# Last stage of a two-layer graph network on Trainium2: three of ten output chunks written by an early store and a later adding transfer

## The chip, the cores and the metric

The kernel runs on one core of one Trainium2 chip. Five engines work side by side and meet through semaphores: TensorE (PE; its weight loads are listed apart as PEld), VectorE (DVE), ScalarE (ACT), GpSimd (POOL) and SyncE (SP), which here only issues transfers. Sixteen DMA engines carry all transfers of the core. The metric is the device time of one execution in microseconds (us), and lower is better.

## The reference

The graph has 1250 nodes of 512 features and 40000 edges. Two residual layers follow each other, cut here to the end of the second, which is what the change touches:

```python
h = max(layernorm(x), 0)
x = x + L0_gnn(h, edges, edge_attr)          # edge MLP, sum over edges, node MLP, affine layernorm
h = max(layernorm(x), 0)
support = (h @ U * s) @ Vt                   # U: 512 x 64, Vt: 64 x 512
gathered = support[src] * edge_weight[:, None]
out = segment_sum(gathered, dst) + bias
x = x + relu(out)
return x                                     # 1250 x 512, fp32
```

## The kernel before, in words

The program is a row of stages, each written once for each engine: a prologue, an edge stage that takes nearly all of the time (to about 1406 us of the trace), a node stage, and a final stage. The 1250 nodes are cut into ten chunks of 128 rows (`NCH` is 10; the last chunk has 98 rows). An engine runs its own part of a stage in the order in which it is written, and waits with `wait_ge` on a semaphore where it needs another engine or a transfer.

The node stage makes `x1`, the input of the second layer, pair of chunks by pair of chunks. `second_norm(p)` on DVE is its last step for the pair p: it raises the semaphore `n_nm` (`s_nm`) by one, after `x1` of chunks 2p and 2p+1 has its final value for this stage. ACT then makes the normed `h2` out of it (L1731), PE multiplies by `U` (L2052) and then by the weighted adjacency `M` (L2065), summed over all ten chunks in two PSUM banks. `M` is loaded from the DRAM table `M_tab` by SP, the last eight chunks of it behind one wait (L1618, tiles `Mb` and `Mc`). When the sum is complete, ACT and DVE copy one half each into the tile `sums` (L1787, L1974).

The final stage computes out = x1 + relu(sums @ Vt + bias) for each chunk. Chunks go in pairs (0,5), (1,6), (2,7), (3,8), (4,9), and `turn` is a chunk's place in that order. PE seeds a PSUM bank with the bias (L2302) and adds the product by `VV` (L2308). Six banks serve the ten turns (`pf`), so the seed of turn 6 waits until the bank of turn 0 has been read, and so on. In `final_stage` DVE takes relu and the sum with `x1` in one instruction (L2292) and SP stores the chunk to `out` (L2327). ACT and GpSimd have nothing to do there.

An adding transfer exists in the kernel already: GpSimd issues `dma_start(..., accum_op=ALU.add)`, which adds the source to what stands at the destination. The edge stage uses it to DRAM (L988, `agg_tab`, 64 KB each; L999, `M_tab`) and the node stage to SBUF (L1663 and L1664, rows of `b4` and `beta` added to the tiles `hb`, `xb`, `uTh_raw` and `ag`). The tile `ag` (four chunks of 128 x 512) is last used in the node stage, for the last pair.

Of the kernel before, what the change touches and what calls it, by code (L numbers as in the profile page):

```python
# [23 lines left out]
ACT = mybir.ActivationFunctionType  # L24
AX = mybir.AxisListType

P = 128
# [3 lines left out]
NCH = -(-N // P)  # L31
# [184 lines left out]
def gnn_two_layers(nc, x, src_idx, dst_rows, src_cols, dst_cols, eaT, ew_cols, W1, b1, W2, b2, W3, b3, W4, b4,  # L216
# [4 lines left out]
    def sem(name):  # L221
        assert name not in names
        names.add(name)
        return ctx.enter_context(nc.semaphore(name))
# [7 lines left out]
    def twice(sb, name, shape):  # L232

        st, sb_raw, _ = scope()
        with st:
            raw = sb_raw(name + "_raw", shape)
        return raw, sb(name, shape, F32R)
# [18 lines left out]
    with ctx:  # L256
# [13 lines left out]
        with st:  # L270
            VV = sb_late("VV", [P, H])
            bhl = sb_late("bhl", [P, H], F32R)
            sums = sb_late("sums", [P, HALFN])
# [11 lines left out]
        with st:  # L285
            V3raw, V3l = twice(sb_late, "V3l", [P, KC, H])
# [4 lines left out]
        ag = sb("ag", [P, 4, H])  # L291
        st, _, ps_node = scope()
        with st:
            pu = [ps_node(f"pu{i}") for i in range(2)]
            pt = [ps_node(f"pt{i}") for i in range(2)]
            pu += [ps_node(f"pu{i}") for i in range(2, 4)]
            po = [ps_node(f"po{i}") for i in range(2)]
        q_w3 = sem("q_w3")
        q_v3 = sem("q_v3")
# [480 lines left out]
        with xst:  # L780
            x1 = sb("x1", [P, NCH, H])
            S = sb("S", [P, NCH, R])
            sel = sb("sel", [P, H], F32R)
            s_sum = sem("k_sum")
            q_v = sem("k_v")
            s_bhl = sem("s_bhl")
            node_stage(node, scope, sem, locals())
            conv_general(c_general, scope, sem, locals())
            final_stage(final, sem, locals())
# [712 lines left out]
def node_stage(work, scope, sem, k):  # L1502
# [3 lines left out]
    ident, iota_p, nTh, nTl, x1, S, sel, ag, q_ag = (  # L1506
        k[n] for n in ("ident", "iota_p", "nTh", "nTl", "x1", "S", "sel", "ag", "q_ag"))
    x, b3, b4, W3, W4, rstd0, nmr0, M_d, Mb, VV, bhl, sums = (
        k[n] for n in ("x", "b3", "b4", "W3", "W4", "rstd", "nmr", "M_d", "Mb", "VV", "bhl", "sums"))
    gamma, beta, U, sv, Vt, bias, row_bcast, newton = (  # L1510
        k[n] for n in ("gamma", "beta", "U", "sv", "Vt", "bias", "row_bcast", "newton"))
    pu, pt, po, xpart, load_ag, s_fin, s_agg, s_t, s_sum, q_v, s_bhl = (
        k[n] for n in ("pu", "pt", "po", "xpart", "load_ag", "s_fin", "s_agg", "s_t", "s_sum", "q_v", "s_bhl"))
    V3raw, V3l, q_v3 = (k[n] for n in ("V3raw", "V3l", "q_v3"))
    NORMS = [(0, 0), (1, 0), (0, 1), (1, 1), (0, 2), (1, 2), (0, 3), (1, 3), (0, 4), (1, 4)]

    st, sb, _ = scope()
    with st:
# [54 lines left out]
        s_ln = sem("n_ln")  # L1573
        s_var = sem("n_var")
        s_r = sem("n_r")
        s_nm = sem("n_nm")
        s_h2 = sem("n_h2")
        s_t2 = sem("n_t2")
        s_e2 = sem("n_e2")
# [682 lines left out]

def final_stage(work, sem, k):

    x1, sums, VV, bhl, sel, out, pu, pt, po, s_sum, q_v, s_bhl = (
        k[n] for n in ("x1", "sums", "VV", "bhl", "sel", "out", "pu", "pt", "po", "s_sum", "q_v", "s_bhl"))
    pf = [pt[0], pt[1], pu[2], pu[3], po[0], po[1]]
    PAIRS = [(i, i + NCH // 2) for i in range(NCH // 2)]
    turn = {c: n for n, c in enumerate(c for pair in PAIRS for c in pair)}
    s_f = sem("k_f")  # L2270
    s_out = sem("k_out")
    q_o = sem("k_o")

    def rows(c):

        return min(P, N - c * P)

    @work.on("scalar")
    def _(e):
        pass  # L2280

    @work.on("gpsimd")
    def _(e):
        pass

    @work.on("vector")
    def _(e):
        for pair in PAIRS:
            for c in pair:
                r = rows(c)  # L2290
                e.wait_ge(s_f, turn[c] + 1)
                e.scalar_tensor_tensor(x1[0:r, c, :], pf[turn[c] % 6][0:r, :], 0.0, x1[0:r, c, :], ALU.max, ALU.add)\  # L2292
                 .then_inc(s_out, 1)

    @work.on("tensor")
    def _(e):
        def seed(pair):
            for c in pair:
                if turn[c] >= 6:
                    e.wait_ge(s_out, turn[c] - 5)  # L2300
                a = R * (c // (NCH // 2))
                e.matmul(pf[turn[c] % 6][0:rows(c), :], sel[a:a + R, 0:rows(c)], bhl[a:a + R, :], start=True, stop=False,  # L2302
                         skip_group_check=True)

        def product(pair):
            for c in pair:
                a, o = R * (c // (NCH // 2)), c % (NCH // 2) * P
                e.matmul(pf[turn[c] % 6][0:rows(c), :], sums[a:a + R, o:o + rows(c)], VV[a:a + R, :], start=False, stop=True,  # L2308
                         skip_group_check=True).then_inc(s_f, 1)

        e.wait_ge(s_bhl, 2)
        e.wait_ge(q_v, 2 * 16)
        for pair in PAIRS[0:3]:
            seed(pair)
        e.wait_ge(s_sum, 2)
        for n, pair in enumerate(PAIRS):
            if n >= 3:
                seed(pair)
            product(pair)

    @work.on("sync")
    def _(e):
        for pair in PAIRS:
            for c in pair:
                r = rows(c)
                e.wait_ge(s_out, turn[c] + 1)
                e.dma_start(out[c * P:c * P + r, :], x1[0:r, c, :]).then_inc(q_o, 16)  # L2327
        e.wait_ge(q_o, 16 * NCH)


# ---- launch: one core; the host only lays the edges out by groups and subtiles
# [32 lines left out]
```

## Time and profile before

| what | us |
|---|---|
| median of 3 runs | 1541.91 |
| lowest and highest of them | 1540.08, 1542.75 |
| the profiled execution, its own time | 1540.79 |
| its span in the trace | 1539.1 |
| PE, DVE, ACT, POOL busy | 1498.8, 1414.7, 1296.5, 1082.4 |

Times in the trace count from the start of the span. An instruction belongs to a line of the kernel (L2292), and `out<-in` names the tiles that it writes and reads. Idle time is shown with what ended it. DMA rows cut a window into 40 equal slices: a digit is the busy share of the 16 DMA engines in tenths, and GB/s is what they moved. Queue q1 holds the transfers that SP issues, q0 those that GpSimd issues.

### The profile page before, as it was taken

Reading aid. Unit: us, or ns where it says so; the run is one execution under the profiler, and the core shown is the slowest. Engines: PE = TensorE matmul, PEld = TensorE weight load, DVE = VectorE, ACT = ScalarE, POOL = GpSimd, SP = SyncE. Lnnn points to the kernel's source line nnn. Section 1 sums busy time; section 2 is a strip of 40 time slices with the busy share of each in tenths; the row PEclk is TensorE's granted clock in tenths of the full one; section 3 lists DMA queues with packets and bytes.
Section 4 is the critical chain, followed back from the end, with each engine's and each line's share of the span. In section 5 each row is a group of like instructions: output and inputs, shape, how many; then the busy total and the mean of one; then the engine's idle time right before and its main releaser. Section 6 shows DMA issues by size and latency. Waiting matters only on the chain.

```text
span 1539.1 us, 33365 instructions
## 1 busy us (share of the span) xinstructions
PE 1498.8 (97%) x7862; PEld 1170.1 (76%) x7862; DVE 1414.7 (92%) x2922; ACT 1296.5 (84%) x2505; POOL 1082.4 (70%) x984
## 2 busy tenths in 40 slices
PE   7969999999999999999999999999999999999998
PEld 5747777777777777777777777777777777776785
DVE  7679999999999999999999999999999999995666
ACT  4058999999999999999999999999999999995462
POOL 1246888888888788787788887888878888762220
PEclk9979999999999999999999999999999999999999
DMA  8845555555554555544554555555555455455673
GB/s 310 306 138 142 125 118 122 124 119 117 124 123 116 123 123 115 127 117 115 126 119 116 127 121 117 121 124 118 118 122 124 116 123 124 112 136 127 137 146 151
DMA packets 122452, 205.10 MB, mean 133 GB/s; under 512 B 31641, under 2 KB 54297, under 8 KB 122416
## 3 DMA queue, kind: packets, MB, share of 16 engines
q0 software_dynamic: 59392, 116.85, 34.8%
q1 hardware_dynamic: 62672, 87.30, 18.2%
q10 hardware_dynamic: 352, 0.52, 0.1%
q8 instruction: 16, 0.26, 0.1%
q14 instruction: 20, 0.16, 0.0%
HBM read 151.60 MB, written 42.75 MB: 126 GB/s over the span
## 4 chain that ended last, share of the span: by engine, by line
PE 81%; issue 5%; DVE 4%; POOL 4%; DMA 3%; ACT 1%; POOLq 1%; DVEq 0%; SPq 0%; ACTq 0%
PE bm L1070 48%; PE bp L1049 6%; PE bp L1057 5%; PE bs L1093 4%; PE bp L1059 4%; PE pu L336 2%; PE pm L1081 2%; PE pu L1998 2%; PE po L2020 2%; PE pB L679 2%; DMA xg<-A_tab,idx 1%; PE pm L1080 1%; POOL hTl L974 1%; POOL M_tab L999 1%; POOL agg_tab L988 1%
## 5 line engine op out<-in xcount | busy, mean ns | idle before, releaser
L974 POOL TENSOR_TENSOR hTl<-tp,hTh 128x512 fp32r<-128x512 f32 (+1 forms) x314 | 411.0, 1309 | 224.5 <-DVE khl L1261 203.5
L1070 PE MATMUL bm<-W2h,hTh 128*128 128x512 f32 x1252 | 498.4, 398 | 2.2 <-POOL hTl L974 1.7
L1070 PE MATMUL bm<-W2l,hTh 128*128 128x512 f32 x1252 | 497.0, 397 | 0.0
L1070 PE MATMUL bm<-W2h,hTl 128*128 128x512 f32 x1252 | 494.5, 395 | 0.0
L963 POOL DMA_INDIRECT xg<-A_tab,idx x305 | 319.4, 1047 | 49.5 <-issue 39.1
L1070 PEld LDWEIGHTS bm<-W2h,hTh 128*128 128x128 f32 x1252 | 235.5, 188 | 71.7 <-DVE bm L1254 14.8
L1131 ACT ACTIVATE rp<-bp 128x512 f32<-128x512 f32 (+1 forms) x314 | 183.3, 584 | 116.8 <-PE bp L1059 115.7
L1070 PEld LDWEIGHTS bm<-W2l,hTh 128*128 128x128 f32 x1252 | 235.6, 188 | 57.5
L1070 PEld LDWEIGHTS bm<-W2h,hTl 128*128 128x128 f32 x1252 | 235.6, 188 | 53.7
L1225 DVE SCALAR_TENSOR_TENSOR rp<-rp 128x512 f32<-128x512 f32 (+1 forms) x314 | 215.6, 687 | 38.7 <-ACT rp L1131 25.8
L1235 DVE SCALAR_TENSOR_TENSOR tp<-rp,bp 128x512 f32<-128x512 f32 (+1 forms) x314 | 211.7, 674 | 4.5 <-ACT rp L1137 2.2
L1248 DVE SCALAR_TENSOR_TENSOR tm<-rm,bm 128x512 f32<-128x512 f32 x313 | 210.5, 673 | 3.4 <-ACT rm L1154 3.4
L1254 DVE COPY bm<-b2b 128x512 f32<-128x512 f32 x309 | 210.7, 682 | 0.0
L1134 ACT ACTIVATE rp<-rp 128x512 f32<-128x512 f32 (+1 forms) x314 | 195.5, 623 | 10.8 <-DVE rp L1225 4.8
L1150 ACT ACTIVATE rm<-rm 128x512 f32<-128x512 f32 x313 | 197.9, 632 | 5.0
L1152 ACT ACTIVATE rm<-rm 128x512 f32<-128x512 f32 x313 | 195.1, 623 | 0.1
L1154 ACT ACTIVATE rm<-rm 128x512 f32<-128x512 f32 x313 | 195.0, 623 | 0.1
L1137 ACT ACTIVATE rp<-rp 128x512 f32<-128x512 f32 (+1 forms) x314 | 194.1, 618 | 0.1
L1146 ACT ACTIVATE rm<-bm 128x512 f32<-128x512 f32 x313 | 185.0, 591 | 1.9 <-DVE tm L1248 1.8
L1049 PEld LDWEIGHTS bp<-ident_r,xg 128*128 128x128 f32 (+1 forms) x1244 | 124.1, 141 | 75.3 <-issue 42.3
L988 POOL DMA_DIRECT2D agg_tab<-ev x157 | 156.4, 996 | 25.2 <-DMA agg_tab<-ev 13.2
L999 POOL DMA_DIRECT2D M_tab<-mev x157 | 163.8, 1044 | 10.1 <-issue 9.2
(244 smaller groups left out, 2318.9 us busy)
## 6 DMA issues: line engine op xcount, KB each, us to landing
ea<-in_eaT SPq DMA_DIRECT2D x156, 128.0 KB
M_tab<-mev POOLq DMA_DIRECT2D x157, 80.0 KB
agg_tab<-ev POOLq DMA_DIRECT2D x157, 64.0 KB
db<-in_dst_rows SPq DMA_DIRECT2D x78, 128.0 KB
M<-M SPq DMA_DIRECT2D x76, 128.0 KB
xg<-A_tab,idx POOLq DMA_INDIRECT x313
eaW<-Bh_tab SPq DMA_DIRECT2D x77, 64.0 KB
eaW<-Bl_tab SPq DMA_DIRECT2D x77, 64.0 KB
```

The lines of the kernel that those rows point to most:

```text
L963: e.indirect_dma_start(out=xg[p][0:r, t, :].bitcast(F32), out_offset=None, in_=A_d, in_offset=bass.IndirectOffsetOnAxis(ap=idx[p][0:r, t:t ...
L974: e.tensor_tensor(hTl[p][:, j, 0:w], pick(u, start_t, tp)[:, 0:w], hTh[p][:, j, 0:w], ALU.subtract)\
L1049: e.matmul(bank[:, t * P:t * P + r].bitcast(F32R), xg[p][0:r, t, j * P:(j + 1) * P], ident_r[0:r, 0:r], start=t == 0, stop=False, is_trans ...
L1070: last = e.matmul(bank[0:r, :], a[p][:, c, j * P:j * P + r], w[:, c, :], start=False, stop=c == KC - 1 and w is W2l, skip_group_check=True)
L1134: e.activation(t, t, ACT.Ln, bias=1.0, scale=0.5 / (SQ * SQ)).then_inc(a_pre, 1)
L1150: e.activation(t, t, ACT.Square, bias=SQ, scale=SQ).then_inc(a_msg, 1)
L1152: e.activation(t, t, ACT.Ln, bias=0.5, scale=0.5 / (SQ * SQ)).then_inc(a_msg, 1)
L1154: e.activation(t, t, ACT.Exp, scale=-1.0).then_inc(a_msg, 1)
L1225: e.scalar_tensor_tensor(t, t, 2.0 * SQ, t, ALU.add, ALU.mult).then_inc(v_sq, 1)
L1235: e.scalar_tensor_tensor(t, pick(u, start_r, rp)[:, 0:w], 1.0, pick(u, start_bank, bp)[:, 0:w], ALU.subtract, ALU.mult).then_inc(v_pre, 1)
L1248: e.scalar_tensor_tensor(tm[m.const % MBUF][0:r, :], rm[m.const % 2][0:r, :], 1.0, bm[m.j][0:r, :], ALU.subtract, ALU.mult).then_inc(v_msg, 1)
L1254: e.tensor_copy(bm[m.j][:, :], b2b[:]).then_inc(v_bias, 1)
```

## The change

For chunks 0, 1 and 2 (`ADDED`) the output is now made in two steps. SP stores `x1` of the three chunks to `out` as it stands, once `n_nm` has reached 2. In the final stage ACT takes the relu of their PSUM banks into the tile `ag`, and GpSimd adds `ag` to `out` with three adding transfers of 256 KB, each behind ACT's relu and the first also behind the landing of the three early stores (`k_x1`). The other seven chunks (`REST`) go as before. A seed that takes over a bank read by ACT waits for ACT instead of DVE.

```diff
+    TURNS = [c for pair in PAIRS for c in pair]
+    ADDED = [0, 1, 2]
+    REST = [c for c in TURNS if c not in ADDED]
...
     @work.on("scalar")
     def _(e):
-        pass
+        for c in ADDED:
+            e.wait_ge(s_f, turn[c] + 1)
+            e.activation(ag[:, c, :], pf[turn[c] % 6][:, :], ACT.Relu).then_inc(s_relu, 1)

     @work.on("gpsimd")
     def _(e):
-        pass
+        e.wait_ge(q_x1, 16 * len(ADDED))
+        for c in ADDED:
+            e.wait_ge(s_relu, c + 1)
+            e.dma_start(out[c * P:(c + 1) * P, :], ag[:, c, :], accum_op=ALU.add).then_inc(q_add, 16)
+        e.wait_ge(q_add, 16 * len(ADDED))
...
     @work.on("tensor")
...
                 if turn[c] >= 6:
-                    e.wait_ge(s_out, turn[c] - 5)
+                    old = TURNS[turn[c] - 6]
+                    if old in ADDED:
+                        e.wait_ge(s_relu, ADDED.index(old) + 1)
+                    else:
+                        e.wait_ge(s_out, REST.index(old) + 1)
...
     @work.on("sync")
     def _(e):
-        for pair in PAIRS:
-            for c in pair:
-                r = rows(c)
-                e.wait_ge(s_out, turn[c] + 1)
-                e.dma_start(out[c * P:c * P + r, :], x1[0:r, c, :]).then_inc(q_o, 16)
-        e.wait_ge(q_o, 16 * NCH)
+        e.wait_ge(s_nm, 2)
+        for c in ADDED:
+            e.dma_start(out[c * P:(c + 1) * P, :], x1[:, c, :]).then_inc(q_x1, 16)
+        for c in REST:
+            r = rows(c)
+            e.wait_ge(s_out, REST.index(c) + 1)
+            e.dma_start(out[c * P:c * P + r, :], x1[0:r, c, :]).then_inc(q_o, 16)
+        e.wait_ge(q_o, 16 * len(REST))
```

DVE's loop runs over `REST` instead of all ten chunks, and is otherwise the same. The rows below are the instructions of an engine in program order; lines marked + have the numbers of the changed kernel, and `k_out` counts DVE's results, `k_relu` ACT's, `k_x1` the landings of the early stores.

SP, from the end of the node stage (the branch of L144) to the end of the program:

```order
 L144 UNCONDITIONAL_BRANCH
-L2327 DMA out<-x 128x512 [waits k_out] x9
-L2327 DMA out<-x 98x512 [waits k_out]
+L2340 DMA out<-x 128x512 [waits n_nm]
+L2340 DMA out<-x 128x512 x2
+L2344 DMA out<-x 128x512 [waits k_out] x6
+L2344 DMA out<-x 98x512 [waits k_out]
 L148 UNCONDITIONAL_BRANCH [waits k_o]
```

Three of SP's ten stores no longer wait for DVE's result; they stand directly behind the loads of `M`, with a wait for `n_nm` alone.

GpSimd, from the end of the node stage to the end of the program (the first rows belong to a branch that is not taken here):

```order
 L2186 DMA h_S<-Sl_tab,h_idx 64x64
 L144 UNCONDITIONAL_BRANCH
+L2295 DMA out<-ag 128x512 [waits k_relu,k_x1]
+L2295 DMA out<-ag 128x512 [waits k_relu] x2
+L148 UNCONDITIONAL_BRANCH [waits k_add]
```

GpSimd gains three transfers and a wait for their landing (`k_add`), ahead of the end of the program.

## Rows read from the trace of the kernel before

**Rows 1.** Chain that ended last, its final pieces: start us, us, what.
```profile
1529.61 4.26 DVE x L2292 x7
...
1534.47 1.20 DVE x L2292 x2
```
**Rows 2.** DMA queues, window 1529 to 1539.1 (the last stage).
```profile
DMA  0000000049999999999999999999999998872000
GB/s 32 0 0 0 0 0 0 0 170 373 389 390 365 406 349 381 381 357 422 357 389 389 365 397 389 381 389 373 397 381 365 381 341 235 260 268 97 0 0 0
q1 hardware_dynamic: 1408, 2.56, 69.9%
```
**Rows 3.** Timeline of the last stage: start us, us, engine, instruction [idle before].
```profile
1528.54 1.02 PE L2308 MATMUL pt<-VV,sums 64*128 64x512 f32 x4
...
1529.59 1.29 DVE L2292 SCALAR_TENSOR_TENSOR x<-pt,x 128x512 f32<-128x512 f32 x2 [1.25 <-PE pt L2308]
1530.25 1.02 PE L2308 MATMUL po<-VV,sums 64*128 64x512 f32 x4
1530.31 5.87 SPq L2327 DMA_DIRECT2D out<-x  x10
...
1532.43 1.04 PE L2308 MATMUL pu<-VV,sums 64*128 64x512 f32 x4
```
**Rows 4.** Windows: us, busy of PE, PEld, DVE, ACT, POOL; then PEclk, DMA share, GB/s.
```profile
1431.00:1436.00 5.00, 5.00 (x31) 4.14 (x30) 3.11 (x6) 4.19 (x8) 1.58 (x2) 1.00 1.09 259
1437.00:1445.00 8.00, 8.00 (x34) 5.92 (x32) 3.68 (x6) 1.92 (x4) 1.30 (x1) 1.00 1.03 187
1474.00:1482.00 8.00, 6.65 (x47) 5.85 (x46) 3.00 (x10) 6.64 (x14) 2.74 (x3) 1.00 1.04 198
1484.50:1490.50 6.00, 6.00 (x42) 5.34 (x41) 3.85 (x12) 0.44 (x3) 0.77 (x1) 1.00 1.04 157
1508.00:1529.00 21.00, 20.71 (x155) 13.37 (x156) 12.17 (x42) 7.85 (x17) 0.00 (x0) 1.00 0.02 8
1531.20:1537.50 6.30, 2.27 (x14) 0.92 (x10) 4.47 (x8) 0.00 (x0) 0.00 (x0) 0.93 1.02 375
```
**Rows 5.** SP's issues before the last stage, and ACT's reads of x of chunks 0 to 3.
```profile
1496.03 2.19 SPq L1618 DMA_DIRECT2D Mc<-M_tab  x4
L1731 ACT ACTIVATE xb<-x,nmr,rstd x4: 802/802/805, 1467.9 to 1474.0; 128x512 f32<-128x512 f32 x4
```
**Rows 6.** Page, part 5: ACT reading a PSUM bank of 128x512.
```profile
L1131 ACT ACTIVATE rp<-bp 128x512 f32<-128x512 f32 (+1 forms) x314 | 183.3, 584 | 116.8 <-PE bp L1059 115.7
```
**Rows 7.** DMA queues (packets, MB, share) in windows 1431:1436, 1437:1445, 1474:1482.
```profile
q0 software_dynamic: 351, 0.72, 78.7%
q1 hardware_dynamic: 127, 0.57, 30.0%
...
q0 software_dynamic: 484, 0.96, 82.6%
q1 hardware_dynamic: 261, 0.51, 19.4%
...
q0 software_dynamic: 572, 1.12, 84.3%
q1 hardware_dynamic: 256, 0.46, 19.4%
```
**Rows 8.** Adding transfers: GpSimd's issue, and issue to landing of agg_tab (to DRAM).
```profile
1482.20 1.19 POOL L1663 DMA_DIRECT2D ag<-in_b  x1 [0.73 <-ACT ag L1701]
...
1483.51 1.76 POOL L1666 DMA_DIRECT2D ag<-in_beta  x1
...
DMA to landing us min/median/max: 4.8/7.6/9.7
```
**Rows 9.** DMA queues, window 1483 to 1492, three adding transfers alone.
```profile
DMA  0000178999799999999899959999999793000000
ag<-in_beta POOLq DMA_DIRECT2D x1, 196.0 KB, 7.6
```

More of the change, by code:

```diff
@@ L786, in gnn_two_layers @@
             s_bhl = sem("s_bhl")
+            s_nm = sem("n_nm")
             node_stage(node, scope, sem, locals())
@@ L1513, in node_stage @@
         k[n] for n in ("pu", "pt", "po", "xpart", "load_ag", "s_fin", "s_agg", "s_t", "s_sum", "q_v", "s_bhl"))
-    V3raw, V3l, q_v3 = (k[n] for n in ("V3raw", "V3l", "q_v3"))
+    V3raw, V3l, q_v3, s_nm = (k[n] for n in ("V3raw", "V3l", "q_v3", "s_nm"))
     NORMS = [(0, 0), (1, 0), (0, 1), (1, 1), (0, 2), (1, 2), (0, 3), (1, 3), (0, 4), (1, 4)]
@@ L1575, in node_stage @@
         s_r = sem("n_r")
-        s_nm = sem("n_nm")
         s_h2 = sem("n_h2")
@@ L2263, in final_stage @@
 def final_stage(work, sem, k):
-    x1, sums, VV, bhl, sel, out, pu, pt, po, s_sum, q_v, s_bhl = (
-        k[n] for n in ("x1", "sums", "VV", "bhl", "sel", "out", "pu", "pt", "po", "s_sum", "q_v", "s_bhl"))
+    x1, ag, sums, VV, bhl, sel, out, pu, pt, po, s_sum, q_v, s_bhl, s_nm = (
+        k[n] for n in ("x1", "ag", "sums", "VV", "bhl", "sel", "out", "pu", "pt", "po", "s_sum", "q_v", "s_bhl", "s_nm"))
     pf = [pt[0], pt[1], pu[2], pu[3], po[0], po[1]]
     PAIRS = [(i, i + NCH // 2) for i in range(NCH // 2)]
-    turn = {c: n for n, c in enumerate(c for pair in PAIRS for c in pair)}
+    TURNS = [c for pair in PAIRS for c in pair]
+    ADDED = [0, 1, 2]
+    REST = [c for c in TURNS if c not in ADDED]
+    turn = {c: n for n, c in enumerate(TURNS)}
     s_f = sem("k_f")
+    s_relu = sem("k_relu")
     s_out = sem("k_out")
+    q_x1 = sem("k_x1")
+    q_add = sem("k_add")
     q_o = sem("k_o")
@@ L2279, in _ @@
     def _(e):
-        pass
+        for c in ADDED:
+            e.wait_ge(s_f, turn[c] + 1)
+            e.activation(ag[:, c, :], pf[turn[c] % 6][:, :], ACT.Relu).then_inc(s_relu, 1)
     @work.on("gpsimd")
     def _(e):
-        pass
+        e.wait_ge(q_x1, 16 * len(ADDED))
[3 more added lines that the diff above has]
+        e.wait_ge(q_add, 16 * len(ADDED))
     @work.on("vector")
     def _(e):
-        for pair in PAIRS:
-            for c in pair:
-                r = rows(c)
-                e.wait_ge(s_f, turn[c] + 1)
-                e.scalar_tensor_tensor(x1[0:r, c, :], pf[turn[c] % 6][0:r, :], 0.0, x1[0:r, c, :], ALU.max, ALU.add)\
-                 .then_inc(s_out, 1)
+        for c in REST:
+            r = rows(c)
+            e.wait_ge(s_f, turn[c] + 1)
+            e.scalar_tensor_tensor(x1[0:r, c, :], pf[turn[c] % 6][0:r, :], 0.0, x1[0:r, c, :], ALU.max, ALU.add)\
+             .then_inc(s_out, 1)
     @work.on("tensor")
@@ L2322, in _ @@
     def _(e):
-        for pair in PAIRS:
-            for c in pair:
-                r = rows(c)
-                e.wait_ge(s_out, turn[c] + 1)
-                e.dma_start(out[c * P:c * P + r, :], x1[0:r, c, :]).then_inc(q_o, 16)
-        e.wait_ge(q_o, 16 * NCH)
+        e.wait_ge(s_nm, 2)
+        for c in ADDED:
+            e.dma_start(out[c * P:(c + 1) * P, :], x1[:, c, :]).then_inc(q_x1, 16)
+        for c in REST:
+            r = rows(c)
+            e.wait_ge(s_out, REST.index(c) + 1)
+            e.dma_start(out[c * P:c * P + r, :], x1[0:r, c, :]).then_inc(q_o, 16)
+        e.wait_ge(q_o, 16 * len(REST))
 def kernel(x, src, dst, edge_attr_64, edge_weight, L0_gnn_W1, L0_gnn_b1, L0_gnn_W2, L0_gnn_b2, L0_gnn_W3,
```

## The prediction

> **What bounds the kernel now.** I read the page's chain first, then the DMA rows of the last stage, then the timeline of that stage, and last the windows in which adding transfers ran. The chain ends in VectorE's ten relu-and-add instructions, seven and two of them listed, back to back from 1529.61 to 1535.67 [rows 1]. That would put the bound on VectorE. The DMA row of the same stretch says otherwise: from about 1531.1 the sixteen engines are full, without a gap, to about 1538, and the last traffic is gone at 1538.3, 0.8 us ahead of the end of the span [rows 2]. In the window 1531.2 to 1537.5 their share is 1.02 at 375 GB/s [rows 4]. The output is 1250 rows of 2048 bytes, 2.56 MB, and that is what queue q1 carried [rows 2]; at 375 GB/s it takes 6.8 us, and 1531.2 plus 6.8 is 1538.0. So the last stage is bound by its stores. VectorE feeds them only a little faster (a 256 KB chunk each 0.61 us, 4.26 over seven) than they drain (0.70 us), and by its last result 1.2 us or so of backlog stands in the queue.
>
> **What the change removes and adds.** Each of the three chunks has 262144 bytes, 786432 in all.
>
> The early stores cost nothing. SP issues its last load of M at 1496.03 plus 2.19 [rows 5]; the three stores stand behind it, and x of chunks 0 to 3 has been read by ScalarE by 1474, so `n_nm` stands at 2 and nothing waits. Their data runs behind the loads of M, in a stretch (1508 to 1529) in which the DMA engines are 2% busy [rows 4]: 786432 at 375 GB/s are 2.1 us of 21. PE's products with M need loads that are ahead of them in the same queue. If they ran in the last stage instead, they would cost these 2.1 us. GpSimd's wait for their landing is over some 15 us before it matters.
>
> ScalarE's relu costs nothing either. It is idle in the last stage but for one copy; reading a PSUM bank takes it 0.58 us [rows 6]. PE finishes the first pair at 1529.56 and the third at 1531.27 [rows 3], the second in between, so ScalarE is done with chunk 0 at about 1530.2, chunk 1 at 1531.0 and chunk 2 at 1531.9. The seeds of turns 6 and 8 then wait for ScalarE instead of VectorE, no later than before. VectorE has seven instructions instead of ten; its last two wait for PE's last pair, which ended at 1533.47 [rows 3], and with 0.61 us for each of them it ends at about 1534.8 instead of 1535.67. This 0.9 us is not on the bound: the stores queue anyway. The first direct store is still that of the first pair, so the data starts at 1531.1 as before.
>
> Removed from the full stretch: 786432 bytes of plain stores, at 375 GB/s 2.1 us.
>
> Added to it: 786432 bytes of adding transfers. The trace has none of 256 KB from SBUF to DRAM, so I bound the price by the windows in which adding transfers to SBUF kept the engines full:
> - alone: 157 GB/s at a share of 1.04 [rows 4], which gives 5.0 us.
> - beside plain 2 KB rows, 1474 to 1482: 1.12 MB added and 0.46 MB plain [rows 7]. The plain part at 375 GB/s takes 1.2 us of the 8, and 6.8 us for 1.12 MB are 165 GB/s: 4.8 us.
> - the same, 1437 to 1445: 0.96 MB added, 0.51 plain; 1.4 us off 8 leaves 6.6, 145 GB/s: 5.4 us.
> - beside the loads of M, 1431 to 1436: 0.72 added, 0.57 plain, 1.5 us off 5 leaves 3.5, 206 GB/s: 3.8 us. This is the lower end from a row.
>
> I take 4.8 us, since its window is nearest: 2 KB rows of both kinds at once. The transfers that GpSimd issues run on the same full engines, so nothing hides them. GpSimd's issues take about 1.2 us and traffic shows 1.7 us after an issue (1482.20 to 1483.9) [rows 8, 9], so the first adding data can come at about 1532; a later start costs only what gaps the direct stores leave, since it is the sum that counts.
>
> The Trainium skill, in "DMA: Bandwidth & Descriptors", section "Issuing engines are not separate DMA queues", says that transfers of all issuing engines run on the same sixteen engines and interleave. That speaks against this change, and the window with both queues full at once agrees. By it the sum is the one above; had GpSimd's queue lanes of its own, the direct stores would end 2.1 us earlier and the adding ones, 4.8 us from 1532, would end at 1536.8, so the stage would gain over 1 us.
>
> The end: a plain store's last traffic stands 0.8 us before the end of the span. The last adding transfer of the node stage, issued at 1483.51, landed 7.6 us later at 1491.1, 0.45 us after the last traffic at 1490.65 [rows 8, 9]; to DRAM I have only landing times, 4.8 us at the least for 64 KB [rows 8], which leaves room for more than 1 us behind the data (4.8 less 1.7 to the first traffic, less 64 KB at 157 GB/s, 0.4, is 2.7). Between -0.3 and +1.9 against now I take +0.3, nearer to the row that was seen.
>
> Sum: -2.1 + 4.8 + 0.3 = +3.0 us. The span goes from 1539.1 to 1542.1, the profiled execution from 1540.79 to 1543.8. Its time stands 1.1 us under the median of 1541.91, so the median after is 1544.9.
>
> **The rivals.** What a measurement of this kernel can tell from no change is about 0.2%, 3.1 us; the forecast sits just inside it.
>
> A, the forecast: adding costs 145 to 165 GB/s, and a tail of 0 to 0.8: -2.1 + 4.8 and -2.1 + 5.4 give +2.7 to +3.3, with the tail +2.4 to +4.1. Chance 0.53.
>
> B, the adding transfers overlap the plain ones as they did beside the loads of M: -2.1 + 3.8, and the tail, +1.4 to +2.3: 1543.6. For it: the share of 1.09 there is the highest of the windows, and here the source is SBUF and each row has a destination of its own. Against: two windows with 2 KB rows show no such gain. Chance 0.20.
>
> C, the other side: an adding packet costs the engine what a plain one does, so that the bytes of the last stage are the same and only VectorE's earlier end is left. It is decided by the price of adding: under 2.1 us for the three chunks (375 GB/s) the stage is no longer than before, and with the backlog gone VectorE's end, 0.9 us earlier, shows. Time: between -0.9 and +0.5, 1541.5. Against: every window with adding transfers alone or in the majority is at 157 to 259 GB/s with full engines. Chance 0.05.
>
> The Trainium skill, same page, section "Anatomy of one DMA — SWDGE (gpsimd) path", fits a transfer issued by GpSimd as 2.0 us plus its bytes over 436 GB/s, with no price for adding. An estimate by that page is 0.6 us of data a chunk, as a plain one, and it gives rival C. The window of adding transfers alone at 157 GB/s speaks against it.
>
> D, slower by more: adding to DRAM is dearer than to SBUF, because each row must be read back first, or its landing comes late. For it: the 64 KB ones of the edge stage took 7.6 us to land, and up to 9.7 [rows 8]. The last of ours is issued at about 1532.1; a landing 9.7 us later, with the other 192 KB at 157 GB/s on top (1.3 us), is 1543.1, +4.0 on the span; the dearest window with the widest tail is -2.1 + 5.4 + 1.9 = +5.2. So about +4.6: 1546.5. Chance 0.22.
>
> **How the numbers follow.** The predicted time is A's, 1544.9. The range leaves out most of C and what lies beyond the dearest sum of D: from +0.5 to +5.6 (0.4 over +5.2, for the spread of the runs), 1542.4 to 1547.5. Slower by over 0.2%: the upper 4 tenths of A (0.22) and all of D, 0.44. Faster by over 0.2% needs more than C can give; 0.03 is left for a shift that has nothing to do with these steps. Within 0.2%: 0.53.
>
> **What the profile after would show.** Right: three `out<-x` stores issued at about 1498 and a DMA burst of 2 us behind the loads of M; three ScalarE relus between 1529.6 and 1532; VectorE ending near 1534.8; in the last stage full DMA engines from 1531.1 to near 1541 with the GB/s falling from 375 to about 260 or less once queue q0 joins; the span ended by the landing of `out<-ag`, on GpSimd. Wrong: a stretch after 1532 at over 350 GB/s with q0 in it (C), a q0 share in a ten-microsecond window far from the 48% that 4.8 us make (B below, D above), or gaps in the DMA row while GpSimd's transfers are under way. The prediction falls too if the early stores delay a product with M, which would show as PE waiting for a DMA before 1527.

## The result, and the profile after

| kernel | median us | lowest to highest | ratio to before (95% interval) |
|---|---|---|---|
| before, 10 runs | 1541.62 | 1538.72 to 1542.75 | |
| changed, 10 runs | 1545.65 | 1544.34 to 1546.99 | 1.0027 (1.0018 to 1.0035) |

The change makes the kernel 4.0 us slower, 0.27%. It was forecast 3.0 us slower, at 1544.9. Two executions among all the runs of this document fell far out of line and are left out of the ratios: one of 1626.56 us at a granted clock of 0.847 (the changed kernel's second set) and one of 4822.73 us, unexplained (the run with plain transfers).

The profiled execution has a span of 1542.7 against 1539.1. That is only 3.6 us more, because in this execution the stages ahead of the last one came through 1.1 us earlier: VectorE's first instruction of the last stage starts at 1528.52, against 1529.59 in [rows 3]. That lead is older than the change: SyncE's loads of `Mc`, which stand ahead of the first changed instruction, are issued from 1494.90 against 1496.03 [rows 5], and in the traces below from 1494.3 to 1499.1. So I count the last stage from that instruction to the end of the span: 9.5 us before (1539.1 less 1529.59), 14.2 after (1542.7 less 1528.52), 4.7 more.

The timeline of the last stage of the changed kernel, cut to ScalarE's and VectorE's instructions and to the issues of SyncE and GpSimd (VectorE's second to fifth of seven and ScalarE's second of three are left out):

```profile
1528.48 0.60 ACT L2288 ACTIVATE ag<-pt 128x512 f32<-128x512 f32 x1 [1.32 <-PE pt L2323]
1528.52 0.69 DVE L2303 SCALAR_TENSOR_TENSOR x<-pt,x 128x512 f32<-128x512 f32 x1 [1.31 <-PE pt L2323]
...
1529.24 6.79 SPq L2344 DMA_DIRECT2D out<-x  x7
...
1529.68 2.69 POOL L2295 DMA_DIRECT2D out<-ag  x3 [31.09 <-ACT ag L2288]
...
1530.20 0.60 ACT L2288 ACTIVATE ag<-po 128x512 f32<-128x512 f32 x1 [0.26 <-PE po L2323]
...
1532.49 1.28 DVE L2303 SCALAR_TENSOR_TENSOR x<-pu,x 128x512 f32<-128x512 f32 x2
```

The compute side did what the text said. ScalarE runs beside VectorE, GpSimd issues 0.6 us after the end of the first relu (1529.08), and VectorE is through 5.25 us after its first start (1533.77), against 6.1 before (1535.67 less 1529.59).

The DMA queues of the changed kernel from 1530 to 1542.7, which answer to [rows 2]; a slice is 0.32 us:

```profile
DMA  7959999999999999999999999999830000000000
GB/s 277 381 174 342 329 200 129 142 181 206 245 387 336 200 245 219 245 271 335 265 219 245 258 265 323 394 413 381 348 110 0 0 0 0 0 0 0 0 0 0
q1 hardware_dynamic: 976, 1.77, 39.3%
q0 software_dynamic: 432, 0.79, 36.7%
```

But for one slice at 5, the engines are as full as before. In that slice, 1530.6 to 1531.0, the first direct chunk is out and the next has not started: PE gives a direct chunk only each 0.86 us here, and a chunk drains in 0.70. From 1531.6 to 1537.6 they move 129 to 271 GB/s in most slices instead of 375. Queue q0 has 0.79 MB and takes 36.7% of 12.7 us, 4.7 us; q1 has 1.77 MB and takes 5.0 us. Together 9.7, where [rows 2] have 69.9% of 10.1, 7.1 us: 2.6 us more. (These are the times of the packets of both queues; they fit into the 9.5 us with data because packets of the two overlap a little: the share of the engines is 1.09 from 1531.2 to 1537.5, against 1.02 before [rows 4].) Per row of 2048 bytes, q0 spends 36.7% of 16 times 12.7 us on 384 rows, 194 ns; q1 before spent 69.9% of 16 times 10.1 us on 1250 rows, 90 ns.

Then the row is empty for ten slices. The last data moves at about 1539.5 and the span ends at 1542.7. The instructions at the end of the program (line 148) say who was awaited. A q behind the engine's name means that its sequencer did it, PEld stands for PE; the numbers are the duration in ns (lowest, median, highest) and the first and last start:

```profile
L148 PEldq DRAIN  x1: 2290/2290/2290, 1530.1 to 1530.1; - x1
L148 ACTq DRAIN  x1: 627/627/627, 1530.2 to 1530.2; - x1
L148 DVEq DRAIN  x1: 1393/1393/1393, 1532.4 to 1532.4; - x1
L148 POOLq DRAIN  x1: 3584/3584/3584, 1538.8 to 1538.8; - x1
L148 SPq DRAIN  x1: 13/13/13, 1540.1 to 1540.1; - x1
L148 SPq EVENT_SEMAPHORE  x1: 17/17/17, 1542.6 to 1542.6; - x1
```

and the same for the kernel before:

```profile
L148 POOLq DRAIN  x1: 3963/3963/3963, 1499.2 to 1499.2; - x1
L148 DVEq DRAIN  x1: 2176/2176/2176, 1533.5 to 1533.5; - x1
L148 SPq DRAIN  x1: 13/13/13, 1538.9 to 1538.9; - x1
L148 SPq EVENT_SEMAPHORE  x1: 17/17/17, 1539.1 to 1539.1; - x1
```

Every engine ends its program with an instruction named DRAIN, and all meet behind it. GpSimd's takes 3.6 us. Before, it stood at 1499.2, when GpSimd had nothing left to do, and was hidden. Now GpSimd waits for the landing of its adding transfers (1538.7), and its DRAIN runs from 1538.8 to 1542.4, 2.3 us past SyncE's at 1540.1. So the 4.7 us have two parts. SyncE is through 11.6 us after VectorE's first start instead of 9.3, 2.3 more; and the span ends 2.6 us behind SyncE's DRAIN instead of 0.2, 2.4 more, which is GpSimd's DRAIN.

The chain that ended last shows neither. Its last piece is VectorE's last instruction, 9 us ahead of the end:

```profile
1533.17 0.60 DVE x L2303
```

The landings of the three adding transfers (GpSimd's instructions on the tile `ag` in the last stage), counted from their issue, the last of which is at 1531.1 (the longest one is that of the last, so it landed at 1538.7):

```profile
DMA to landing us min/median/max: 4.5/6.3/7.6
```

### The profile page after: what moved, and what is told of

The parts are those of the page before. It is cut to its first block, busy times and chain, and to the rows that moved or that the text cites. A ratio compares the mean times of both kernels' runs of the same rounds, so it can differ in the third digit from the quotient of the medians.

```text
span 1542.7 us, 33370 instructions
## 1 busy us (share of the span) xinstructions
PE 1500.1 (97%) x7862; PEld 1172.1 (76%) x7862; DVE 1412.2 (92%) x2919; ACT 1298.2 (84%) x2508; POOL 1084.0 (70%) x987
## 4 chain that ended last, share of the span: by engine, by line
PE 82%; issue 5%; DVE 4%; POOL 4%; DMA 2%; POOLq 1%; ACT 1%; DVEq 0%; SPq 0%; ACTq 0%
PE bm L1071 47%; PE bp L1050 6%; PE bp L1058 5%; PE bs L1094 4%; PE bp L1060 4%; PE pu L336 2%; PE pm L1082 2%; PE pu L1998 2%; PE po L2020 2%; PE pB L679 2%; DMA xg<-A_tab,idx 1%; PE pm L1081 1%; POOL hTl L975 1%; PE pA L679 1%; POOL M_tab L1000 1%
## 5 line engine op out<-in xcount | busy, mean ns | idle before, releaser
L1000 POOL DMA_DIRECT2D M_tab<-mev x157 | 162.5, 1035 | 10.1 <-issue 9.2
```

## The experiments

The theory after the result: two costs, adding (2.3 us, in the DMA engines) and GpSimd's DRAIN (2.4 us, at the end of the program). Each run's stage length is read from its own trace as above. Each ratio is to the kernel before, run on the same chip as the run itself: its median there was 1540.30 us for the first four runs and 1541.49 for the last four, so a median below and its ratio are not to be set against 1541.62.

### SyncE waits for the adding transfers, not GpSimd

```diff
     @work.on("gpsimd")
...
-        e.wait_ge(q_add, 16 * len(ADDED))
...
     @work.on("sync")
...
         e.wait_ge(q_o, 16 * len(REST))
+        e.wait_ge(q_add, 16 * len(ADDED))
```

> The changed kernel, but SyncE and not GpSimd waits for the landing of the three adding transfers. Theory: in the changed kernel the adding transfers have landed at 1538.7, SyncE is through at 1540.1, and the end comes only at 1542.6 because GpSimd, which waited to the last, then spends 3.6 us in the DRAIN at the end of its program. With the wait on SyncE that DRAIN begins when the last issue is made, at about 1532.5, ends by about 1536 and is hidden: 2.4 us less than the changed kernel, some 1.6 us (0.1%) over the kernel before. Rival: the DRAIN is long because GpSimd's own transfers are under way or have just landed; then it only stretches to their landing and 3.6 us more, and the time stays at the changed kernel's, 4 us over before.

Measured: 1544.01 us median, ratio 1.0021 (1.0013 to 1.0030). VectorE's first instruction of the last stage in its timeline:

```profile
1531.43 0.69 DVE L2302 SCALAR_TENSOR_TENSOR x<-pt,x 128x512 f32<-128x512 f32 x1 [1.29 <-PE pt L2322]
```

and at the end of its program:

```profile
L148 POOLq DRAIN  x1: 8866/8866/8866, 1534.0 to 1534.0; - x1
L148 SPq DRAIN  x1: 13/13/13, 1543.0 to 1543.0; - x1
```

The stage is 11.9 us long (1543.3 less 1531.43), 2.3 shorter than in the changed kernel. The detail of the theory was wrong: the DRAIN is not over by 1536. It starts at 1534.0 and lasts 8.9 us, to 1542.9, 1.4 us behind the last landing (the third transfer, issued at 1534.0, landed 7.5 us later). It does stretch, as the rival said, but to 1.4 us behind the landing and not 3.6. So it ends 0.1 us ahead of SyncE, which is held by the direct stores: level with it, but not setting the end.

### The same, with GpSimd's transfers plain

```diff
-            e.dma_start(out[c * P:(c + 1) * P, :], ag[:, c, :], accum_op=ALU.add).then_inc(q_add, 16)
+            e.dma_start(out[c * P:(c + 1) * P, :], ag[:, c, :]).then_inc(q_add, 16)
```

> As the run with SyncE's wait, but GpSimd's three transfers overwrite instead of add, so chunks 0 to 2 of the output are relu alone, without x. Bytes, queue and issue are the same, only the adding is gone. Theory: an adding row of 2 KB takes a DMA engine 192 ns instead of 89, so the three chunks cost 4.6 us instead of 2.1, and this run is 2.4 us faster than the one with SyncE's wait and within 0.5 us of the kernel before. Rival: the price is that of GpSimd's queue (descriptors written by software, late start) and not of adding; then nothing is gained over the run with SyncE's wait.

Measured: 1540.86 us, ratio 1.0002 (0.9993 to 1.0011). Its DMA queues from 1529 to 1545, a slice being 0.4 us:

```profile
GB/s 0 0 0 20 0 0 0 0 0 333 323 246 399 333 333 399 369 369 379 435 313 369 399 374 384 256 287 103 0 0 0 0 0 0 0 0 0 0 0 0
...
q0 software_dynamic: 240, 0.79, 13.2%
```

VectorE's first instruction of the stage:

```profile
1531.10 0.69 DVE L2302 SCALAR_TENSOR_TENSOR x<-pt,x 128x512 f32<-128x512 f32 x1 [1.31 <-PE pt L2322]
```

and at the end of its program:

```profile
L148 POOLq DRAIN  x1: 5486/5486/5486, 1533.6 to 1533.6; - x1
L148 SPq DRAIN  x1: 13/13/13, 1540.7 to 1540.7; - x1
```

The same 0.79 MB on the same queue take 13.2% of 16 us, 2.1 us, instead of 4.7. The stage is 9.8 us long (1540.9 less 1531.10), within 0.3 of before and 2.1 shorter than with SyncE's wait; in the ratios it is 0.19%, 2.9 us. The price is that of adding, not of GpSimd's queue. Nor is it that of the packet size alone: the adding rows go in packets of 2 KB, the plain ones of GpSimd in packets of 4 KB, but SyncE's plain rows go in packets of 2 KB too and take 90 ns each. The run says a second thing: VectorE has seven instructions here as in the changed kernel, and the stage gains nothing by it. The DMA engines are the bound.

### The kernel before, with GpSimd waiting to the end

```diff
     @work.on("gpsimd")
     def _(e):
-        pass
+        e.wait_ge(q_o, 16 * NCH)
```

> The kernel before, with one wait more: GpSimd, which has nothing to do in the last stage, also waits for all ten stores. No transfer is changed. Theory: GpSimd's DRAIN of 3.2 to 3.6 us, hidden at 1499 in the kernel before, now begins at about 1538.7 and sets the end: 3.2 to 3.5 us (0.2%) slower than before. Rival: DRAIN is short where GpSimd has no transfer or instruction of its own just behind it; then the time is that of the kernel before within 0.3 us.

Measured: 1545.51 us, ratio 1.0033 (1.0021 to 1.0046), for one wait and no transfer. In its timeline:

```profile
1530.98 1.29 DVE L2292 SCALAR_TENSOR_TENSOR x<-pt,x 128x512 f32<-128x512 f32 x2 [1.25 <-PE pt L2308]
```

and at the end of its program:

```profile
L148 POOLq DRAIN  x1: 3339/3339/3339, 1540.3 to 1540.3; - x1
L148 SPq DRAIN  x1: 13/13/13, 1540.3 to 1540.3; - x1
L148 SPq EVENT_SEMAPHORE  x1: 17/17/17, 1543.8 to 1543.8; - x1
```

The stage is 12.8 us long (1543.8 less 1530.98), 3.3 more than before, as expected and against the rival: the DRAIN takes 3.3 us though GpSimd had no instruction for some 40 us and no transfer in the stage. The lower end of the interval is 3.2 us; the 5 us of the ratio's middle are more than the trace shows.

### The kernel before, with the early stores added

```diff
     @work.on("sync")
     def _(e):
+        e.wait_ge(s_nm, 2)
+        for c in (0, 1, 2):
+            e.dma_start(out[c * P:(c + 1) * P, :], x1[:, c, :]).then_inc(q_x1, 16)
+        e.wait_ge(q_x1, 3 * 16)
...
     @work.on("vector")
     def _(e):
+        e.wait_ge(q_x1, 3 * 16)
```

> The kernel before with the three early stores of x added (and SyncE and VectorE waiting for their landing ahead of the last stage); the last stage still stores all ten chunks. Theory: the early stores run behind the loads of M in a stretch with idle DMA engines and cost nothing: same as before within 0.5 us. Rival: they delay the loads of M or something behind them: 1 to 2 us slower.

Measured: 1541.21 us, ratio 1.0006 (0.9997 to 1.0015); the stage is 9.5 us long (1539.3 less 1529.76), as before. The interval reaches to 2.3 us, so the times alone don't exclude the rival's 1 to 2 us. The traces do. SyncE's last loads ahead of the early stores, the early stores and the stores of the last stage stand in its timeline as

```profile
1496.12 2.27 SPq L1618 DMA_DIRECT2D Mc<-M_tab  x4
1498.62 1.33 SPq L2327 DMA_DIRECT2D out<-x  x3
1530.52 5.86 SPq L2333 DMA_DIRECT2D out<-x  x10
```

From the first of these loads to the first store of the last stage there are 34.40 us here, 34.28 before (1496.03 to 1530.31, [rows 3, 5]) and 34.34 in the changed kernel (1494.90 to 1529.24). The early stores cost about 0.1 us in the trace.

### The changed kernel and SyncE's wait once more, side by side

> The changed kernel once more, on the chip and beside the runs of the next one, since the two were 2.4 us apart in their traces and only 0.9 us apart in ratios taken on different days of the chip. Theory: 4.0 to 4.7 us over the kernel before, 2.3 us over the same kernel with SyncE's wait. Rival: GpSimd's DRAIN costs at most 1 us of time, and the two stand within 1 us.

> The changed kernel with the landing of the adding transfers waited for by SyncE, a second time. Theory: 2.1 to 2.5 us (0.15%) over the kernel before: what is left is the price of adding alone, and GpSimd's DRAIN, which stretches to 1.4 us behind the last landing, ends with SyncE. Rival: as the changed kernel, within 1 us.

Measured: changed kernel 1545.78 us, 1.0027 (1.0018 to 1.0037), stage 14.0 us (1541.9 less 1527.94); with SyncE's wait 1544.51, 1.0018 (1.0009 to 1.0027), stage 11.8 (1544.2 less 1532.42):

```profile
L148 POOLq DRAIN  x1: 3584/3584/3584, 1538.1 to 1538.1; - x1
L148 SPq DRAIN  x1: 13/13/13, 1539.4 to 1539.4; - x1
```

for the changed kernel, and with SyncE's wait

```profile
L148 POOLq DRAIN  x1: 8847/8847/8847, 1535.0 to 1535.0; - x1
L148 SPq DRAIN  x1: 13/13/13, 1544.0 to 1544.0; - x1
```

Both pairs of traces put the stages of the two 2.2 to 2.3 us apart. The ratios put them 0.06% and 0.09% apart, 0.9 and 1.4 us, with intervals that overlap. In the second pair, on one chip, the means of the executions differ by 1.3 us, with a 95% interval of about 0 to 2.6, which holds the 2.3 and the rival's 1 alike. That GpSimd's DRAIN sets the end of the changed kernel is shown by the traces and by the kernel before with one wait; whether the median moves by the whole 2.3 us or by half of it isn't settled by these times.

### One chunk added, and four

```diff
-    ADDED = [0, 1, 2]
+    ADDED = [0]
```

> As the run with SyncE's wait, but one chunk (0) is added instead of three. Theory: an added chunk costs the sixteen engines 8 rows each at 192 ns instead of 89, 0.8 us, so the time is 0.8 us over the kernel before. Rival: most of the cost is a fixed one of the first adding transfer (start and completion); then it stays near the 2.3 us of three chunks.

```diff
-    ADDED = [0, 1, 2]
+    ADDED = [0, 1, 2, 3]
```

> As the run with SyncE's wait, but four chunks (0 to 3) are added instead of three. Theory: 0.8 us more than with three, 3.2 us over the kernel before. Rival, a fixed cost: as with three, 2.3 us over it.

Measured: one chunk 1542.20 us, 1.0001 (0.9992 to 1.0010); four chunks 1545.53 us, 1.0023 (1.0014 to 1.0033). From the traces, with SyncE's DRAIN as the mark for the end of the transfers:

```profile
1530.70 0.69 DVE L2302 SCALAR_TENSOR_TENSOR x<-pt,x 128x512 f32<-128x512 f32 x1 [1.29 <-PE pt L2322]
```

and at the end of its program:

```profile
L148 SPq DRAIN  x1: 13/13/13, 1541.2 to 1541.2; - x1
```

for one chunk, and for four

```profile
1532.74 0.69 DVE L2302 SCALAR_TENSOR_TENSOR x<-pt,x 128x512 f32<-128x512 f32 x1 [1.29 <-PE pt L2322]
```

and at the end of its program:

```profile
L148 POOLq DRAIN  x1: 9152/9152/9152, 1536.4 to 1536.4; - x1
L148 SPq DRAIN  x1: 13/13/13, 1545.0 to 1545.0; - x1
L148 SPq EVENT_SEMAPHORE  x1: 17/17/17, 1545.7 to 1545.7; - x1
```

SyncE is through 9.3, 10.5, 11.6 and 12.3 us after VectorE's first start with none, one, three and four chunks added. That is 1.2 us for the first chunk, 0.55 for each of the next two and 0.7 for the fourth, 0.75 on average, where 0.8 each was expected. So the theory holds for the sum and not for the first chunk, which is dearer in its one trace; why stays open. The ratio of one chunk has 1.5 us as its upper end, so the rival's fixed cost of 2.3 us is out. The times of four chunks (1.0023, 2.2 to 5.1 us) don't tell 3.2 us from the rival's 2.3; there only the trace speaks against it. With four chunks the last landing is so late that GpSimd's DRAIN (to 1545.6) ends behind SyncE even where SyncE does the waiting, and adds 0.6 us again.

## Why the prediction was right, and where it was not

**The bound.** Right. The last stage is bound by its stores: with GpSimd's transfers plain, VectorE's earlier end was worth nothing. VectorE ended 5.25 us after its first start; the text's 1534.8 less 1529.59 is 5.2.

**The early stores, ScalarE's relu, the seeds.** Right at nothing. Early stores alone cost 0.1 us in the trace, ScalarE starts its third relu 0.04 us after PE's third pair is done, and no seed waits longer: PE starts that of turn 6 2.2 us after its first product in both kernels.

**The price of adding.** Right in mechanism and near in size. The text took 4.8 us for 786432 bytes, from the window in which adding and plain 2 KB rows shared the engines [rows 4, 7]; queue q0 took 4.7 us. Net of the plain stores it said +2.7; q0 and q1 together took 2.6 us more, and SyncE came through 2.3 us later. In a window of ten microseconds q0's share is 47%, where the text had 48%. The overlap of rival B did not show beyond these few tenths, and rival C's plain price is what the transfers cost when they don't add. The Trainium skill's fit in "DMA: Bandwidth & Descriptors", section "Anatomy of one DMA — SWDGE (gpsimd) path", has no price for adding: by it an estimate for a landing of 256 KB is 2.6 us. The trace agrees at the low end for the plain ones, which landed 2.8 to 4.1 us after their issue beside the direct stores; the adding ones took 4.3 to 7.6 in the changed kernel's two traces.

**The end.** This is the step that failed, the term +0.3. "Between -0.3 and +1.9 against now I take +0.3" reckoned with the landing of the last adding transfer alone. That landing was no problem: it came at 1538.7, ahead of the direct stores. What was overlooked is that GpSimd gets a last wait and has a DRAIN of more than 3 us behind it. The trace of before had it, 3963 ns at 1499.2, hidden by 36 us. It is worth 2.3 to 2.4 us in the traces, above the text's upper bound of 1.9, and 0.9 to 2.4 with the ratios taken in. "The span ended by the landing of `out<-ag`, on GpSimd" was right only in the engine: GpSimd ended it, and the span was over 4.0 us after that landing.

**The number.** That 1544.9 came within 0.8 us of the median is in part luck. By the traces the sum is +2.3 for adding and +2.4 for the DRAIN, 4.7, where the text had +2.7 and +0.3; the medians moved 0.7 us less than the traces. The measured +4.0 is at the upper edge of the forecast case (+2.4 to +4.1). Rival D had about that time (+4.0 to +5.2), by a late landing that did not happen.

**The chances.** The text gave 0.53 to a change within 0.2% (3.1 us) and 0.44 to slower by more, and it was slower by more. With SyncE's wait, so without the DRAIN, the ratios are 1.0021 and 1.0018, at that line.

**Slips in the sums.** The forecast case names a tail of 0 to 0.8, but its +2.4 needs -0.3. Rival B's upper end with the same 0.8 is +2.5, not +2.3. Neither moves the forecast or the range.

No version here beats the kernel before. The best of those that add is the one with a single chunk: equal within 1.5 us by its times, 1.2 us longer in its trace. The bytes of the last stage are the bound, and adding moves them at less than half the rate (194 ns a row instead of 90).

## What to carry to other kernels

Storing a part early and adding the rest later saves no bytes at the end, and a row added by a transfer held a DMA engine twice as long as a row stored. So by these numbers it can pay only where the DMA engines have room at the end; no run here has such a place. Before giving an idle engine the last wait of a program, look at what it does behind its last instruction: here the end of GpSimd's program costs 3.3 us or more, and a wait that SyncE can take should be taken by SyncE (2.3 us in the traces here, 0.9 to 1.4 in the ratios). The chain of waits ended in VectorE both times and showed neither the full DMA engines nor the DRAIN; the DMA row and the last instructions of each engine did.

## What the runs showed of the hardware

- GpSimd's DRAIN at the end of the program takes 3.3 us behind a bare wait (with no transfer of its own), 3.6 us behind adding transfers that have landed, and with three transfers under way it lasts to 1.3 or 1.4 us behind the last landing (8.9 and 8.8 us long with adding ones, 5.5 with plain ones). SyncE's takes 13 ns, ScalarE's 0.3 to 0.6 us, VectorE's 1.3 to 2.2. What GpSimd does in these microseconds no run shows. The Trainium skill, "VectorE: DVE Perf Modes", section "The DRAIN you can't avoid", knows DRAINs that the runtime puts ahead of and behind a kernel, about 12 ns each on all five engines. Those here stand at line 148 of the kernel itself and need not be the same; SyncE's 13 ns is near that figure, GpSimd's 3.3 us is not.
- An adding transfer from SBUF to DRAM costs a DMA engine 194 ns per 2 KB row (the changed kernel), a plain one 90 ns (the kernel before), and the adding ones to SBUF were near the 194 (157 GB/s over sixteen engines, [rows 4], which is 209 ns a row).
- GpSimd's plain transfers of 2 KB rows came as 240 packets for the 0.79 MB, the adding ones as 432. Both counts hold 48 small ones, 16 for each of the three transfers, so the plain data went in packets of 4 KB (192) and the adding in packets of 2 KB (384); in rate the plain ones were no better for it than SyncE's (13.2% of 16 times 16 us over 384 rows is 88 ns a row, against 90).
- SyncE's own issues got longer with GpSimd's transfers in the engines: 0.33 to 0.49 us each before, up to 1.5 us in the changed kernel, up to 1.1 with plain transfers, up to 0.65 with four chunks added. In the changed kernel its last issue ends at 1536.0, 2.3 us behind VectorE's end, instead of 0.5. The engines stayed full meanwhile; why the issues stretch, and whether it costs anything, no run here separates.
